# Output weights' parts made in the first stage, and six output tiles computed in the last head's turns

## What is computed

```
q, k, v = silu(causal_dwconv(x @ Wq)), ... Wk, ... Wv      # 4 taps; k scaled by 128 ** -0.5
alpha, beta = sigmoid(x @ Wa + ba), sigmoid(x @ Wb + bb)
S = alpha * S - beta * (S k - v) k^T;  o = S q              # step by step over 2048 tokens
o = (o - mu) * rsqrt(var + 1e-5) * ln_w + ln_b
out = (o * sigmoid(x @ Wg)).reshape(B, T, H * DV) @ Wo
```

## Time and profile before

| | us |
|---|---|
| median of 3 runs | 3699.24 (3695.61 to 3699.66) |
| the profiled execution | 3697.9 |
| its span, first to last instruction | 3696.3 |
| `prepare`, about | 0 to 475 |
| `heads`, about | 476 to 3325 |
| `project`, about | 3325 to 3696 |
| busy PE / DVE / ACT / POOL | 3563 / 2394 / 2316 / 1950 |

### The profile page before, as it was taken

The page is one execution under the profiler, slowest core; times in us unless marked ns, Lnnn a source line. Parts: engine busy times, 40 slices in busy tenths (PEclk is TensorE's granted clock), DMA queues, the critical chain, the costliest instruction groups (busy, mean ns, idle before and its releaser), DMA issues. The chain is left out here.

```text
span 3696.3 us, 105770 instructions
## 1 busy us (share of the span) xinstructions
PE 3563.1 (96%) x32416; PEld 2937.1 (79%) x32416; DVE 2394.2 (65%) x5756; ACT 2315.8 (63%) x6401; POOL 1949.7 (53%) x4898
## 2 busy tenths in 40 slices
PE   7999969999999999999999999999999999978999
PEld 5777757888888888888888888888888888857887
DVE  4444436777777777777777777777777777743222
ACT  3334437777777777777777777777777777742111
POOL 3344425666665666666666666666666666630000
PEclk9999989999999999999999999999999999979999
DMA  4333343333323333333443233333333333316543
GB/s 153 118 133 122 123 139 70 74 82 77 76 74 84 76 75 80 91 76 74 128 122 77 74 85 76 73 81 78 76 74 90 83 74 80 76 35 187 152 138 113
DMA packets 420101, 348.43 MB, mean 94 GB/s; under 512 B 190449, under 2 KB 323569, under 8 KB 415729
## 3 DMA queue, kind: packets, MB, share of 16 engines
q1 hardware_dynamic: 417008, 333.60, 34.0%
q0 software_dynamic: 2560, 8.39, 0.6%
HBM read 273.75 MB, written 68.16 MB: 93 GB/s over the span
## 5 line engine op out<-in xcount | busy, mean ns | idle before, releaser
L1135 DVE SCALAR_TENSOR_TENSOR conv<-bank,tap,conv 128x512 f32<-128x512 f32 x1152 | 861.6, 748 | 146.6 <-ACT conv L1272 120.4
L971 POOL TENSOR_TENSOR prods<-Lb,Tc 128x60 f32<-128x60 f32 (+14 forms) x1920 | 479.8, 250 | 620.0 <-DMA Lb<-base_d 476.7
L1334 PE MATMUL bank<-hx_hi,w_lo 128*128 128x512 f32 x1536 | 647.2, 421 | 24.2 <-DVE Tnb L1097 22.8
L1334 PE MATMUL bank<-hx_hi,w_hi 128*128 128x512 f32 x1536 | 666.0, 434 | 0.0
L1334 PE MATMUL bank<-hx_lo,w_hi 128*128 128x512 f32 x1536 | 638.5, 416 | 0.0
L978 POOL TENSOR_TENSOR Tc<-Tc,prods 128x56 f32<-128x56 f32 (+13 forms) x1792 | 459.5, 256 | 142.3 <-POOL prods L971 3.6
L1253 ACT ACTIVATE Wc<-bank 128x128 f32<-128x128 f32 x512 | 140.8, 275 | 363.0 <-PE bank L1416 334.8
L1334 PEld LDWEIGHTS bank<-hx_hi,w_lo 128*128 128x128 f32 x1536 | 292.5, 190 | 64.3 <-DVE Tnb L1097 28.5
L1334 PEld LDWEIGHTS bank<-hx_hi,w_hi 128*128 128x128 f32 x1536 | 291.9, 190 | 37.6
L1334 PEld LDWEIGHTS bank<-hx_lo,w_hi 128*128 128x128 f32 x1536 | 292.5, 190 | 32.0
L1089 DVE SCALAR_TENSOR_TENSOR S<-S,gamma,bank 128x128 f32<-128x128 f32 x480 | 166.7, 347 | 228.2 <-PE bank L1427 214.9
(11 more groups left out here) (164 smaller groups left out, 9088.8 us busy)
## 6 DMA issues: line engine op xcount, KB each, us to landing
Lb<-base_d SPq DMA_DIRECT2D x128, 512.0 KB, 4.8
gamma<-gamma_d SPq DMA_DIRECT2D x128, 258.0 KB, 3.6
alpha<-alpha_d SPq DMA_DIRECT2D x128, 256.0 KB, 3.2
oT_d<-oG SPq DMA_DIRECT2D x128, 256.0 KB, 4.7
o_raw<-oT_d SPq DMA_DIRECT2D x32, 1024.0 KB, 6.9
gu_raw<-in_gate_up SPq DMA_DIRECT2D x16, 1408.0 KB, 6.2
w_raw<-in_Wk SPq DMA_DIRECT2D x33, 256.0 KB, 4.6
w_raw<-in_Wq SPq DMA_DIRECT2D x33, 256.0 KB, 4.9
```

The lines of the kernel that those rows point to most:

```text
L971: pool.tensor_tensor(prods[:, :, i + 1:], Lb[:, i, :, i + 1:], Tc[:, :, i:i + 1].to_broadcast([P, G, SB - 1 - i]), ALU.mult)\
L1135: dve.scalar_tensor_tensor(out=conv[i][:, to], in0=PJ[PJ_OF[g][i]][:], scalar=tap[:, i, j + 1:j + 2], in1=conv[i][:, to], op0=ALU.mult, op ...
L1334: last = pe.matmul(dst, a[:, i, k], b[:, k], start=(j == 0), stop=(j == 3 * KC - 1))
```

## The change

It has three parts.

**Wo's parts in the first stage.** `prepare` now loads Wo in four parts of four heads (1 MB each) into `w_raw`, cuts each behind the third hidden block of experts 0 to 3 (`wo_high`: four ACT copies of 128 x 512; `wo_low`: four POOL subtractions), and stores the parts into four more slots of `xT_hi_d` and `xT_lo_d`. The second turn of experts is written out instead of looped.

**Six output tiles in the last head's turns.** After the last projection from each group of x, SP loads Wo's parts into that group's tiles `x_hi[g]`, `x_lo[g]`. In the turns of the last head and two turns behind them, `out_some` makes tiles 4 to 9 of batch 0 (48 matmuls each) where projections stood. The cuts of `oT_d` take the places of weight cuts (`w_raw`, `w_hi`, `w_lo`), DVE adds x in the unused `conv` tiles, and SP stores. `project` starts with its first tile cut and Wo's parts in place, and makes 26 tiles.

**First loads of `heads` in another order**, and ACT's wait for `ln_w` and `ln_b` moved from its start to the first use.

```diff
+TILES, TILE0 = 6, 4
+TILE_CUT_AT = {20: (0, 1), 26: (1, 1), 33: (2, 1), 4: (3, 0)}
+TILE_AT = 2
...
+                wait(sp, wo_lo_done, 4 * r)
+                sp.dma_start(w_raw[:].rearrange("p k c d -> p k (c d)"), wo_rows[r]).then_inc(wo_loaded, 16)
+
+            def store_wo(r):
+                for part, done, dst in ((w_hi, wo_hi_done, xT_hi_d), (w_lo, wo_lo_done, xT_lo_d)):
+                    wait(sp, done, 4 * r + 4)
+                    sp.dma_start(dst[NG + r], part[:].bitcast(F32).rearrange("p k c d -> p k (c d)")).then_inc(wo_stored, 16)
+
             load_x(0)
...
+            load_wo(0)
             load_expert(1)
             load_expert(2)
+            store_wo(0)
+            load_wo(1)
+            wait(sp, xn_done, TT)
+            load_expert(3)
+            load_x(1)
+            store_wo(1)
+            load_wo(2)
+            load_expert(4)
+            store_wo(2)
+            load_wo(3)
+            store(1)
+            wait(sp, xn_done, 2 * TT)
+            load_expert(5)
+            load_x(2)
+            store_wo(3)
...
+            def wo_low(r, blocks):
+                for i in blocks:
+                    wait(pool, wo_stored, 32 * r)
+                    wait(pool, wo_hi_done, 4 * r + i + 1)
+                    pool.tensor_tensor(w_lo[:, i], w_raw[:, i], w_hi[:, i].bitcast(F32), ALU.subtract)\
+                        .then_inc(wo_lo_done, 1)
...
+                        if wo and m == NM - 1:
+                            wo_low(e, range(4))
...
+            def wo_high(r, blocks):
+                for i in blocks:
+                    wait(act, wo_stored, 32 * r)
+                    wait(act, wo_loaded, 16 * r + 16)
+                    act.activation(w_hi[:, i], w_raw[:, i], ACT.Copy).then_inc(wo_hi_done, 1)
...
+                        if wo and m == NM - 1:
+                            wo_high(e, range(4))
...
+                turn(eng, NH - 1, g, 4 + g, True, g < 3, g < 2, g < 1, False, True, tile=g)
+            turn(eng, NH, 0, 8, False, False, False, False, False, True, tile=4)
+            for g in (1, 2):
+                turn(eng, NH, g, 8 + g, False, False, False, False, False, False, tile=4 + g)
...
+            def load_tile(j):
+                cols = slice((TILE0 + j) * P, (TILE0 + j + 1) * P) if j < TILES else slice(0, P)
+                for i in range(NPROJ):
+                    sp.wait_ge(wlo_done, (NH + j - 2) * NPROJ + i + 1)
+                    sp.dma_start(w_raw[:, i], oT[0, :, KC * i:KC * i + KC, cols]).then_inc(w_loaded[i], 16)
+
+            def load_xt(j):
+                sp.dma_start(conv[j % 3][:, 0:GT], x_rows[(TILE0 + j) * P:(TILE0 + j + 1) * P, :]).then_inc(xt_loaded[j % 3], 16)
+
+            def store_y(j):
+                sp.wait_ge(y_done, j + 1)
+                sp.dma_start(out_rows[(TILE0 + j) * P:(TILE0 + j + 1) * P, :], conv[j % 3][:, 0:GT]).then_inc(y_stored[j % 3], 16)
+
+            def next_tiles(tile):
+                if tile == 0:
+                    sp.wait_ge(silu_done, NH * GROUPS * 3)
+                    for j in range(3):
+                        load_xt(j)
+                else:
+                    store_y(tile - 1)
+                if tile < TILES:
+                    load_tile(tile + 1)
+                if 0 < tile < TILES - 2:
+                    sp.wait_ge(y_stored[(tile - 1) % 3], 16 * ((tile - 1) // 3 + 1))
+                    load_xt(tile + 2)
+
...
+                    sp.wait_ge(proj_done, NPROJ * ((b_next * H - 1) * GROUPS + x_next + 1))
+                    load_x(b_next, x_next)
...
+                if isinstance(hh, int) and hh == NH - 2 and g == 1:
+                    sp.wait_ge(o_stored, 16 * H * GROUPS)
+                    load_tile(0)
...
+                if tile is not None:
+                    next_tiles(tile)
...
-            load_tap(0)
             load_beta(0, 0)
             load_alpha(0, 0)
+            load_tap(0)
             load_x(0, 1)
-            sp.dma_start(lnw[:], ln_w).then_inc(ln_loaded, 16)
-            sp.dma_start(lnb[:], ln_b).then_inc(ln_loaded, 16)
             load_beta(0, 1)
             load_alpha(0, 1)
-            for i in range(NPROJ):
-                load_w(i, 1)
             load_x(0, 2)
-            load_gamma(0, 0)
-            load_scale(0, 0)
-            load_x(0, 3)
 
...
+                    load_x(0, 3)
                     sp.wait_ge(tap_copied, 1)
                     load_tap(1)
+                if n == 1:
+                    for i in range(NPROJ):
+                        load_w(i, 1)
+                    load_gamma(0, 0)
+                    load_scale(0, 0)
+                    sp.dma_start(lnw[:], ln_w).then_inc(ln_loaded, 16)
+                    sp.dma_start(lnb[:], ln_b).then_inc(ln_loaded, 16)
             for g in range(GROUPS):
...
+            next_tiles(4)
             sp.wait_ge(oG_done, NH * GROUPS)
             sp.dma_start(oT_d[NH - 1, :, 3 * GT:4 * GT], oG[:]).then_inc(o_stored, 16)
+            next_tiles(5)
+            next_tiles(6)
+            for i in range(3):
+                sp.wait_ge(y_stored[i], 16 * (TILES // 3))
...
+                    if tile and s == TILE_AT:
+
+                        dve.wait_ge(proj_done, (NH * GROUPS + tile) * NPROJ)
+                        dve.wait_ge(xt_loaded[(tile - 1) % 3], 16 * ((tile - 1) // 3 + 1))
+                        y = conv[(tile - 1) % 3][:, 0:GT]
+                        dve.tensor_tensor(y, PJ[(tile - 1) % 3][:], y, ALU.add).then_inc(y_done, 1)
...
-            act.wait_ge(ln_loaded, 32)
...
+                        if isinstance(hh, int) and hh == 0 and g == 1:
+                            act.wait_ge(ln_loaded, 32)
...
+                    if tile is not None and s in TILE_CUT_AT:
+
+                        i, j = TILE_CUT_AT[s][0], tile + TILE_CUT_AT[s][1]
+                        if 0 < j <= TILES:
+                            act.wait_ge(proj_done, (NH * GROUPS + j - 1) * NPROJ + i + 1)
+                            cut_high(i, (NH + j) * 16)
...
+                def out_some(pieces):
+
+                    for _ in range(pieces):
+                        i, j = divmod(sent[0], 3 * KC)
+                        k, part = divmod(j, 3)
+                        sent[0] += 1
+                        if j == 0:
+                            if i == 0:
+                                wait(pe, y_done, tile - 2)
+                                pe.wait_ge(conv_done, (NH * GROUPS - 1) * 9 + (9 if tile else 3))
+                                if tile:
+                                    pe.wait_ge(tanh_done, NH * GROUPS)
+                            pe.wait_ge(x_loaded[i], (B + 1) * 32)
+                            pe.wait_ge(wlo_done, (NH + tile - 1) * NPROJ + (i + 1))
+                        a, b = ((w_hi, x_hi[i]), (w_hi, x_lo[i]), (w_lo, x_hi[i]))[part]
+                        last = pe.matmul(PJ[tile % 3][:], a[:, i, k], b[:, k], start=(i == 0 and j == 0),
+                                         stop=(i == NPROJ - 1 and j == 3 * KC - 1))
                         if j == 3 * KC - 1:
                             last.then_inc(proj_done, 1)
...
-        wo_raw = sb("wo_raw", [P, H, HID])
-        wo_hi = sb("wo_hi", [P, H, HID], F32R)
-        wo_lo = sb("wo_lo", [P, H, HID], F32R)
-        o_raw = sb("o_raw", [P, 2, H, P])
-        o_hi = sb("o_hi", [P, 2, H, P], F32R)
-        o_lo = sb("o_lo", [P, 2, H, P], F32R)
+        def tile_of_heads(tile):
+            return tile[:].rearrange("p i k d -> p (i k) d")
+
+        o_raw = [tile_of_heads(w_raw), sb("o_raw", [P, H, P])[:]]
+        o_hi = [tile_of_heads(w_cut[0]), sb("o_hi", [P, H, P], F32R)[:]]
+        o_lo = [tile_of_heads(w_cut[1]), sb("o_lo", [P, H, P], F32R)[:]]
         x_t = sb("x_t", [P, 2, HID])
         y = sb("y", [P, 2, HID])
...
+            turn(0, 0, 0, begun=True)
+            turn(1, 0, 1)
+            with sp.Fori(MOE_PAIRS, T // P // 2 - DONE) as j:
+                turn(j, 0, j + DONE)
+            with sp.Fori(T // P // 2 - DONE, PAIRS) as j:
+                turn(j, 1, j - (T // P // 2 - DONE))
```

More of the change, by code:

```diff
@@ L292, in _ @@
             wait(sp, ab_stored, NG * 64)
+            wait(sp, wo_stored, GROUPS * 32)
         @block.gpsimd
@@ L346, in turn @@
                         low(j, range(TT))
-            turn(0, group=False)
-            with pool.Fori(1, END) as j:
+            turn(0, group=False, wo=True)
+            turn(1, wo=True)
+            with pool.Fori(2, END) as j:
                 turn(j)
@@ L506, in turn @@
                         gates(j)
-            turn(0, group=False)
-            with act.Fori(1, END) as j:
+            turn(0, group=False, wo=True)
+            turn(1, wo=True)
+            with act.Fori(2, END) as j:
                 turn(j)
@@ L957, in _, with turn @@
             pool.wait_ge(compact_built, 2)
-            def turn(pool, hh, g, n, chain, late, mid, inv, proj, ln):
+            def turn(pool, hh, g, n, chain, late, mid, inv, proj, ln, tile=None):
```

(16 more changed lines are left out.)

120 lines of the change are left out of this document (60 added, 60 removed).

## The result

The changed kernel takes 3679.3 us (median, 3677.7 to 3680.1) against 3699.5 (3695.6 to 3707.5) for the kernel before in the same session: a ratio of 0.9941, 95% interval 0.9927 to 0.9956. That is 20 us, where 51 were predicted, and outside the range of 3637 to 3662. The profiled execution has a span of 3678.5 us against 3696.3.

A forecast was written before the change was run, and what follows sets the result against it. PE was taken to bound the kernel, busy 3563 of 3696 us, with its few waits. From 3697.9, +7.5 (first stage), -10.5 (start of `heads`) and -48.6 (tail) gave 3646.3, so 3648 us at the median; range 3637 to 3662.

The forecast's parts named there:

- Part 1: First stage: cutting Wo's parts makes PE's path late at experts 0 to 2, plus loads; +7.5 us (5 to 14).
- the third of POOL's ends at 79.6, so `gu_lo` is 0.5 us later still: First stage: `gu_lo`, ready at 79.10, waits for one POOL subtraction; path late by 2.2 us, three times, +6.7 us.
- a whole subtraction each time: First stage, upper bound of the collision: `gu_lo` waits 1.28 us more at each of three experts, 8.9 us in all.
- The term for ACT's copies: First stage: four copies (2.18 us) ahead of `gu_hi`, less 0.46 slack, 1.7 us late at three experts: 5.1 us.
- rival B: Tail: handoffs of tiles 4, 5, 6 and `project`'s first loaded tile are late; 3656 to 3666, say 3660; chance 0.15.
- Part 2: Start of `heads`: ACT starts earlier and the first group's store and load go quicker; -10.5 us (7 to 11.6 gained).
- Part 3: Tail: six output tiles fill the last head's turns, leaving 26 for `project`; -48.6 us (bounds -57 and -36).
- the stretch of the turns: Tail, last projection to last stage: six tiles, 33.4 us of other PE work, idle and handoff; some 102 us.
- ACT's copies and POOL's subtractions stand where the weight cuts stand in other heads: Tail: part of the claim that each tile's handoff fits; ACT's copies are put at 0.55 us.
- C: Start of `heads` gives some 3 us only, as tap or beta land late; 3655 us; chance 0.08.
- D: First stage: Wo's parts land late and ACT holds `gu_hi`; 3655 to 3675, say 3663 us; chance 0.09.
- F: Slower than before: ACT's wait for Wo's part, behind stores on SP's queue, holds `gu_hi` and PE; chance 0.02.

The follow-up runs named there:

- gap kernel: Changed kernel plus one wait: POOL, behind the four `w_lo` subtractions, waits for DVE's `gu_lo` before `dn_lo`; 3650.8 us in one execution.
- The split: Changed kernel with Wo's cuts two and two behind hidden blocks 0 and 1, loads and stores to match; 3640.3 us, 0.9848 to the kernel before.
- the kernel with POOL behind: Changed kernel with only POOL's four Wo subtractions moved behind the next expert's `dn_lo`, ACT and SP as they were; 3656.1 us in one execution.
- step 16: The split, with the first part of the next output tile in the tail's turns cut at step 16 instead of 20, not for tile 0's turn; 3638.1 us.

## Why the prediction was wrong

**Part 1 failed, and it alone takes the time out of the range.** +7.5 was predicted, +37.7 measured. The step is this one: "the third of POOL's ends at 79.6, so `gu_lo` is 0.5 us later still". It took for granted that a waiting `gu_lo` gets in when the POOL instruction in progress ends, and its upper bound, "a whole subtraction each time", rests on the same thought, so the range didn't hold the case either. In truth `gu_lo` was kept out until POOL's row ended: the rest of the four subtractions, then `dn_lo`, and behind expert 3 four of x more. `gu_lo` took 5.0 us more behind three experts and 9.9 more behind the fourth. The gap kernel shows this by itself. The split shows that the hold, and not the work, was the price.

There are rows for which the thought is true, and the prediction leaned on them. DVE's four small scans in the earlier trace rows take 5.06 us, and one at a time, with the POOL instruction beside it, they look like this in the kernel before:

```profile
423.57 1.44 DVE L389 TENSOR_TENSOR_SCAN gam<-ab,zero 16x128 f32<-16x128 f32 x1
...
423.36 1.37 POOL L353 TENSOR_TENSOR w_lo<-w_raw,w_hi 128x512 fp32r<-128x512 f32 x1
```

The scan ends at 425.01, 0.28 us after `w_lo` (424.73), while POOL's next subtraction is already running. Each of these scans waits for one instruction of POOL's row, as each `on` in the tail does. The step that failed is to carry this over to `gu_lo`, for which no row of the kernel before shows a row of POOL in front. What makes the difference is not shown: `gu_lo` is long (3.09 us alone) where the scans and `on` are short (0.39 and 0.34), but they differ in more than that, and no run varied it.

The Trainium skill, SBUF — State Buffer, section "SBUF: two separate sides", says that whichever of the two starts first has the port pair for its whole instruction while the other is blocked. The rows agree that it is no sharing: 8.13 and 13.02 us, where 3.09 is the time alone. For `gu_lo` they go further than that sentence: the blocked one stayed out over the following instructions of the same engine too, as long as these came without a gap.

Two smaller things are missing in Part 1. "Behind expert 3 PE has transposes and the gates' product as well, which hide it" is true of ACT's copies alone (no stall there in the kernel with POOL behind), but not of a hold of 9.9 us: a fourth stall stood there, the longest, 8.10 us. And no clock was charged, though the prediction did charge it for the last stage: each stall was followed by matmuls at half the clock, some 2.5 us each time. The term for ACT's copies was right: 5.0 us of stalls for 5.1. One small sum is off as well, without effect: the load and the two cuts of an o tile, 6.0, 1.9 and 2.3 us, are 10.2 as in rival B, not 10.7.

**Part 2 was right** in mechanism and size: -10.3 against -10.5; undone alone it costs it again (33.9 us), done alone it gives 11.3.

**Part 3 was right in its mechanism, and 6.8 us too large** (-41.8 against -48.6). The turns ran at full clock (0.83 in the first ten us, 1.00 in most windows after), each handoff was in time, the gap was 3.7 us, the last 26 tiles took 284.8 us for 285.6. The term that was off is the stretch of the turns, 109.8 us for 102.2. 5.3 of that is the wait for `on`, behind one to three POOL instructions in a row, each of which holds up one `on`. "ACT's copies and POOL's subtractions stand where the weight cuts stand in other heads" is the failed step: it asks whether POOL finds the time, not whom it keeps waiting. At step 20, where the tiles' first part is cut, DVE has `on` to do, and in the turns just before the tail those groups take 1.1 us, at most 2.3. The rest, 2.4 us, is PE's own work (100.6 busy, 98.2 predicted); the first ten us at 0.83 of the clock make about 1.6 of it (with step 16, where the whole stretch had the full clock, PE is busy 98.9).

The rivals didn't come in. No handoff was late (B), the start of `heads` gave all (C), ACT never waited for Wo's parts (D and F). None of them had what happened, that four subtractions on an engine that is 54% busy hold up one that PE waits for.

With its placement mended, the same change gives 3640 us, 57 under the kernel before; the parts then are 0.1, -10.7 and -41.6 us, and most of the rest is the loop's spread.

## What to carry to other kernels

Before work is put on POOL beside a DVE instruction on the critical path, count the whole row that POOL can run without a gap from that moment, not only the instruction in progress. A long DVE instruction like `gu_lo` may wait for the end of the row; short ones like `on` waited for one POOL instruction each, which also adds up when there are several. Put such rows where DVE has nothing urgent, in small portions, or give POOL a wait on DVE's result in the middle of the row; here one added wait made the first stage 19 us shorter. And price a long stall of PE with the matmuls at half clock behind it, some 2.5 us after each of the stalls of 3.2 to 8.1 us in the changed kernel and the one with the gap, not only with its own length.

## What was unexpected of the hardware

A DVE subtraction of 3.09 us took 8.13 and 13.02 us beside gapless rows of POOL, each time ending 2.95 us after the row, though in the meantime POOL went from one instruction to the next two and six times. Short DVE instructions fared otherwise beside the same kind of row: each TENSOR_SCALAR from SBUF to SBUF, 128x128 with two per-row operands (0.34 us alone), ended 0.08 or 0.09 us after one POOL instruction, and each scan of 16x128 (0.39 us alone) 0.28 us after one, while POOL's next was already running.
